# Destination rows gathered beside the first pass of a two-layer graph network, and half of the dense centring on ScalarE

## What is computed

```python
edge_index = jnp.stack([src, dst])
h = jnp.maximum(_layernorm(x), 0.0)
# layer 0: edge features of h[src] times a small net of the edge, summed per dst;
# cos(angle) * (self product of h) + sin(angle) * (sum through lin2)
x = x + _L0_gnn_ref(h, node_vec1, edge_attr_4, edge_attr_8, ..., src, dst, 16)
h = jnp.maximum(_layernorm(x), 0.0)
# layer 1: edge messages of h[src], summed per dst, one more product, relu
x = x + _L1_gnn_ref(h, edge_attr_4, ..., edge_index)
```

## Time and profile before

| | us |
|---|---|
| median of three runs | 2462.75 |
| the profiled execution | 2464.93 |
| its span, first to last instruction | 2463.1 |

### The profile page before, as it was taken

One profiled execution on the slowest core, in us unless ns is written; L12 is line 12 of the kernel. 1 busy time (PEld: TensorE's weight loads), 2 busy tenths in 40 slices (PEclk: granted clock), 3 DMA queues, 4 the chain that ended last, 5 costly groups with the idle time before them and its releaser, 6 DMA issues. The chain is left out here.

```text
span 2463.1 us, 51415 instructions
## 1 busy us (share of the span) xinstructions
PE 1773.9 (72%) x12130; PEld 1620.2 (66%) x12130; DVE 1866.4 (76%) x6716; ACT 1350.1 (55%) x3801; POOL 1483.3 (60%) x1436
## 2 busy tenths in 40 slices
PE   6788888888888888888886544545444777777776
PEld 2777777777777777777775544444444666666665
DVE  1799999999999999999996766666664555656554
ACT  2466666666666666666665645555553444444443
POOL 2345455454555545555454777777776777767775
PEclk9999999999999999999998555555555999999999
DMA  5355555555555555555554333333333333333332
GB/s 184 128 188 206 200 192 193 185 205 200 195 194 184 203 200 198 194 182 202 200 201 165 118 107 113 113 116 121 116 107 93 99 97 105 108 102 109 108 105 72
DMA packets 162656, 376.27 MB, mean 153 GB/s; under 512 B 42142, under 2 KB 72092, under 8 KB 162462
## 3 DMA queue, kind: packets, MB, share of 16 engines
q1 hardware_dynamic: 115582, 301.58, 34.7%
q0 software_dynamic: 47040, 74.31, 11.4%
HBM read 182.72 MB, written 200.80 MB: 156 GB/s over the span
## 5 line engine op out<-in xcount | busy, mean ns | idle before, releaser
L651 POOL TENSOR_TENSOR yo<-x,h 128x640 f32<-128x640 f32 x196 | 303.7, 1550 | 506.0 <-ACT h L774 504.8
L985 PE MATMUL bank<-wp,hT 128*128 128x160 f32 x1568 | 376.3, 322 | 0.0
L774 ACT ACTIVATE h<-x,nmr,inv 128x160 f32<-128x160 f32 x784 | 342.1, 514 | 1.5 <-DVE nmr L1211 1.5
L985 PE MATMUL bank<-wp,eT 128*128 128x160 f32 x784 | 263.6, 429 | 49.9 <-ACT eR L897 43.7
L610 POOL DMA_INDIRECT out<-yo,i_put x196 | 209.1, 1067 | 119.2 <-issue 80.7
L604 POOL DMA_INDIRECT x_e<-in_xa,i_src x196 | 217.3, 1109 | 98.7 <-issue 47.2
L1354 DVE SCALAR_TENSOR_TENSOR x<-bank,scl,x_all 128x160 f32<-128x160 f32 x784 | 256.3, 365 | 5.1 <-PE bank L986 2.6
L610 POOL DMA_INDIRECT h_all<-h,i_put x196 | 223.9, 1142 | 59.8 <-issue 58.6
L986 PE MATMUL bank<-wp,hR 128*128 128x64 f32 x1568 | 259.3, 247 | 0.0
L986 PEld LDWEIGHTS bank<-wp,hR 128*128 128x128 f32 x1568 | 255.5, 190 | 0.0
L980 PE MATMUL bank<-ident,h_e 128*128 128x128 f32 x392 | 83.6, 351 | 223.4 <-DVE hr_e L1526 223.0
(11 more groups left out here) (163 smaller groups left out, 5537.8 us busy)
## 6 DMA issues: line engine op xcount, KB each, us to landing
x_all<-in_xa SPq DMA_DIRECT2D x98, 644.0 KB, 5.0
h_all<-h SPq DMA_DIRECT2D x98, 640.0 KB, 3.0
out<-yo SPq DMA_DIRECT2D x98, 640.0 KB, 3.4
q_row<-row_tab SPq DMA_DIRECT2D x98, 256.0 KB, 3.6
sum_tab<-tot SPq DMA_DIRECT2D x49, 322.0 KB, 4.2
y_tab<-yo SPq DMA_DIRECT2D x49, 320.0 KB
x<-y_tab SPq DMA_DIRECT2D x49, 320.0 KB
cv<-sum_tab SPq DMA_DIRECT2D x25, 322.0 KB, 3.1
```

Source lines behind the costliest of these rows:

```text
L651: nc.gpsimd.tensor_tensor(yo[j][:, a:b], x1[j][:, a:b], h1[j][:, a:b], ALU.add).then_inc(d_y, 1)
L774: ins = nc.scalar.activation(h1[j][:, k * D:(k + 1) * D], x1[j][:, k * D:(k + 1) * D], ACT.Relu, bias=nmr2[j][:, k:k + 1], scale=inv2[j][: ...
L985: nc.tensor.matmul(dst_ps, main[:, t * P:(t + 1) * P], wp[:, w:w + D], start=True, stop=False)
```

## The change

- The destination rows are gathered in the first pass: GpSimd's odd step ends with `own_gather(q-1)`, four indirect DMAs into x_d (two buffers), and SP stores them to a table own_tab in DRAM (`own_store`). In the second stage SP loads a quad from own_tab (`p2_own`), and GpSimd scatters only. The indices are copied by VectorE at the end of its odd steps of the first pass, not in the second stage.
- The sum of a tile goes to bank 5 or 6 in place of bank 1, so `dense_tr`, `p1_tr` and `p1_sum` lose their waits for each other's copies; `p1_source` now waits for the copy of the sum four tiles back, `p1_sum` for the features of the tile before it in the order.
- Of each dense unit, the 128 last columns of row groups 4 to 7 are centred on ScalarE (four activations, mean minus x; the copy of that half into hT turns the sign back), the rest stays on VectorE.
- `dense_y` makes four sums of 320 columns in place of two of 640.

```diff
 # SP
+            def own_store(q):
+                j = q.mod(2)
+                sp.wait_ge(o_g[j], q.over(2, 64, 64))
+                sp.dma_start(own_tab[q.times(1)], x_d[j][:, :]).then_inc(o_st[j], 16)
...
                 if v.mod(2) == 1 and (q - 2).within(Q):
                     p1_store(q - 2)
+                    own_store(q - 2)
...
+            def p2_own(q):
+                k = q.mod(4)
+                wait(sp, r_x1, q.times(2, -6))
+                sp.dma_start(x_q[k], own_tab[q.times(1)]).then_inc(r_g[k], 16)
 # GpSimd
+            def own_gather(q):
+                j = q.mod(2)
+                pool.wait_ge(o_ix, q.times(1, 1))
+                wait(pool, o_st[j], q.over(2, 16))
+                gather(xa, x_d[j], XW, i_dst[j], o_g[j])
...
-                    a, b = h * GQ * D, (h + 1) * GQ * D
-                    nc.gpsimd.tensor_tensor(yo[j][:, a:b], x1[j][:, a:b], h1[j][:, a:b], ALU.add).then_inc(d_y, 1)
+                    for k in (2 * h, 2 * h + 1):
+                        a, b = 2 * k * D, 2 * (k + 1) * D
+                        ins = nc.gpsimd.tensor_tensor(yo[j][:, a:b], x1[j][:, a:b], h1[j][:, a:b], ALU.add)
+                    ins.then_inc(d_y, 1)
...
                 if w.mod(2) == 1 and (q + 1).within(Q):
                     p1_centre(q + 1)
                     p1_scale(q + 1)
+                if w.mod(2) == 1 and (q - 1).within(Q):
+                    own_gather(q - 1)
 # ScalarE
+            def dense_centre(u):
+                act.wait_ge(d_ln1, u.times(1, 1))
+                wait(act, d_tr, u.times(2, -2))
+                x, st = x_in[u.mod(4)], st1[u.mod(4)]
+                for k in range(GQ, GD):
+                    ins = nc.scalar.activation(hb[u.mod(2)][:, k * P:(k + 1) * P], x[:, k * XW + 32:k * XW + D], ACT.Identity,
+                                               bias=st[:, k, 1:2], scale=-1.0)
+                ins.then_inc(d_cna, 1)
...
-                nc.scalar.activation(hT[h][:, :], bank[0][:, :], ACT.Relu)
+                nc.scalar.activation(hT[h][:, :], bank[0][:, :], ACT.Relu, scale=-1.0 if h else 1.0)
...
                     dense_root1(u)
+                    dense_centre(u)
                 slot(u, 0)
 # TensorE
                 pe.wait_ge(d_cen, u.times(1, 1))
+                if h:
+                    pe.wait_ge(d_cna, u.times(1, 1))
                 wait(pe, d_hT, u.times(2, h))
-                wait(pe, e_tot, u.times(2, h - 2))
...
                 wait(pe, e_ft, n.times(1, -1))
+                wait(pe, e_tot, n.times(1, -3))
                 b = bank[5 + n.mod(2)]
...
-                wait(pe, d_hT, dense_copied)
+                pe.wait_ge(e_ft, n.times(1, 3) if (n + 2).within(T) else T)
+                total = bank[5 + n.mod(2)][:, 0:CW]
 # VectorE
-                V.tensor_tensor(x3(hb[j], P, GD), x[:, :, 32:D], bc_last(stat(st1[u.mod(4)], GD, 1), P), ALU.subtract)
+                V.tensor_tensor(x3(hb[j], P, GD)[:, 0:GQ, :], x[:, 0:GQ, 32:D], bc_last(stat(st1[u.mod(4)], GQ, 1), P),
+                                ALU.subtract)
...
+                if u.mod(2) == 1 and (q1 - 1).within(Q):
+                    wait(v, o_g[(q1 - 1).mod(2)], (q1 - 1).over(2, 64))
+                    index_copy(i_dst[(q1 - 1).mod(2)], t_gat, q1 - 1, o_ix)
```

More of the change, by code:

```diff
@@ L90, in gnn_kernel @@
     row_tab = scratch("row_tab", (T, P), i32)
+    own_tab = scratch("own_tab", (Q, P, GQ * XW))
     carry_tab = scratch("carry_tab", (T, P))
@@ L189, in gnn_kernel @@
         i_src = two("i_src", [P, GQ], i32)
-        i_dst = four("i_dst", [P, GQ], i32)
+        i_dst = two("i_dst", [P, GQ], i32)
         i_put = four("i_put", [P, GQ], i32)
@@ L197, in gnn_kernel @@
         x_e = two("x_e", [P, GQ * XW])
+        x_d = two("x_d", [P, GQ * XW])
         h_e = sb("h_e", [P, GQ * P])
@@ L266, in gnn_kernel @@
         d_sq1 = sem("dense_root1_ready")
-        d_cen = sem("dense_centred")
+        d_cen = sem("dense_first_half_centred")
+        d_cna = sem("dense_second_half_centred")
         d_tr = sem("dense_h_transposed")
@@ L305, in gnn_kernel @@
         e_st = sem2("p1_sum_stored")
-        r_ix = sem("p2_index_copied")
+        o_ix = sem("own_index_copied")
+        o_g = sem2("own_rows_gathered")
+        o_st = sem2("own_rows_stored")
         r_px = sem("p2_put_copied")
         r_cv = [sem(f"p2_sums_loaded{i}") for i in range(4)]
-        r_g = [sem(f"p2_node_rows{i}") for i in range(4)]
+        r_g = [sem(f"p2_own_rows_loaded{i}") for i in range(4)]
         r_ln1 = sem("p2_moments1")
@@ L517, in _ @@
                 sp.wait_ge(e_st[j], 16 * ((Q + 1 - j) // 2))
+                sp.wait_ge(o_st[j], 16 * ((Q + 1 - j) // 2))
+            sp.wait_ge(d_x1, 4 * U)
+            def p2_own(q):
+                k = q.mod(4)
+                wait(sp, r_x1, q.times(2, -6))
+                sp.dma_start(x_q[k], own_tab[q.times(1)]).then_inc(r_g[k], 16)
             def p2_sums(q):
@@ L529, in p2_step @@
             def p2_step(v):
+                if v.within(Q):
+                    p2_own(v)
                 if (v - 1).within(Q):
@@ L692, in _ @@
                 step(At(0, w))
[L695 to L699, removed]
             def p2_scatter(q):
@@ L706, in p2_scatter @@
                     scatter_tile(h1_all, h1[j][:, t * D:(t + 1) * D], i_put[q.mod(4)], t, r_put[j])
[L709 to L717, removed]
             for j in range(2):
@@ L720, in _ @@
                 pool.wait_ge(d_sto[j], 16 * (U // 2))
-            with pool.Fori(1, Q // 4) as i:
+            with pool.Fori(0, Q // 4) as i:
                 for c in range(4):
-                    p2_step(At(i, c))
-            for w in range(Q - 1, Q + 4):
-                p2_step(At(0, w))
+                    p2_scatter(At(i, c))
+            p2_scatter(At(0, Q - 1))
             for j in range(2):
@@ L1064, in p1_source, with p1_sum @@
                                  start=True, stop=True).then_inc(e_pw, 1)
-            def p1_sum(n, dense_copied):
+            def p1_sum(n):
                 j, t = n.c // GQ % 2, n.mod(4)
@@ L1072, in p1_sum @@
                 wait(pe, e_tot, n.times(1))
-                wait(pe, d_hT, dense_copied)
+                pe.wait_ge(e_ft, n.times(1, 3) if (n + 2).within(T) else T)
+                total = bank[5 + n.mod(2)][:, 0:CW]
                 before = tot[j][:, (t - 1) * CW:t * CW] if t else tot[1 - j][:, (GQ - 1) * CW:GQ * CW]
-                nc.tensor.matmul(bank[1][:, U_SEG:U_SEG + CW], same[j][:, t * P:(t + 1) * P], v_e[n.mod(2)][:, :],
+                nc.tensor.matmul(total, same[j][:, t * P:(t + 1) * P], v_e[n.mod(2)][:, :],
                                  start=True, stop=False)
-                nc.tensor.matmul(bank[1][:, U_SEG:U_SEG + CW], carry[j][:, t * P:(t + 1) * P], before,
+                nc.tensor.matmul(total, carry[j][:, t * P:(t + 1) * P], before,
                                  start=False, stop=True).then_inc(e_seg, 1)
@@ L1103, in slot @@
                 if (s - 3).within(T):
-                    p1_sum(s - 3, u.times(2, h) if u.within(U) else 2 * U)
+                    p1_sum(s - 3)
             def step(u):
@@ L1514, in p2_stats @@
                 j = q.mod(2)
-                v.wait_ge(r_g[q.mod(4)], q.over(4, 64, 64))
+                v.wait_ge(r_g[q.mod(4)], q.over(4, 16, 16))
                 for pair in range(GQ // 2):
@@ L1663, in p2_step @@
                     p2_angle(q, 7)
-            for q in range(3):
-                index_copy(i_dst[q], t_gat, At(0, q), r_ix)
             v.wait_ge(d_y, 2 * U)
```

6 lines of the change are left out of this document (1 added, 5 removed).

## The result

The changed kernel takes 2445.51 us (median of six runs, 2438.85 to 2457.62) where the kernel before takes 2463.86 on the same chip: a ratio of 0.9935, 95% interval 0.9918 to 0.9952. So it is 18 us faster, and the forecast of 2408 gave 55. The profiled execution has a span of 2443.7 us.

What follows compares the result with a forecast made beforehand. It took a loop per pair through GpSimd, VectorE, TensorE and ScalarE to bound the first pass, and GpSimd the second stage. 2463.1 - 143.8 + 84 + 5.5 = 2408.8, + 1.8 - 2.2 = 2408 us; range 2335 to 2485.

Steps and rivals of the forecast that it cites:

- Second stage: GpSimd's gathers there give way to straight loads on SP's queue, a step takes 7.6 us: -143.8 us.
- rival C: Second stage held at 9 us a step by SP's loads or ScalarE's table loads: +62, 2470 us; chance 0.07.
- GpSimd decides: First pass: own gathers delay `yo`, for which VectorE's x1 waits: +1.8 us a pair, +84 us.
- The leg: GpSimd's stretch per pair, from `yo` before centring to `yo` after the gathers: from 12.45 to 17.45 us.
- The way back: First pass, from x1 over features, TensorE, hT and h to `yo`: from 12.65 to 9.87 us a pair.
- rival B: The way back keeps its length through ScalarE's new activations: +4.55 us a pair, 2538 us; chance 0.12.
- Rival A: First pass: GpSimd gets through its gathers, other engines stay the limit, a unit takes 12.25 us: 2269 us; chance 0.10.
- Centring on ScalarE: First pass: takes 0.53 us a unit off VectorE and gives ScalarE 1.6 us a unit.
- the ring: First pass, closed chain per pair of GpSimd's leg, x1 and the way back: from 25.62 to 27.4 us.
- rival D: First pass: VectorE's subtractions stretch two more gathers a pair, the leg 1.6 us longer: +75, 2483 us; chance 0.05.
- The half-sized `yo`: First pass: each sum split into two of 320 columns pays start-up twice, +0.3 us on the leg.
- The ends: End of the first pass and SP's first load of the second stage: VectorE starts later, +5.5 us.

Runs made afterwards that it cites:

- e7: The kernel before with only the dense part of the change, destination rows still gathered in the second stage: 2326.8 us, 0.9444 of before.
- e3: The changed kernel plus 32 unused transposes on TensorE in even steps, before the product that waits for x1: 2378.5 us, 0.9660 of before.
- e2: The changed kernel with all centring back on VectorE, ScalarE's four activations gone: 2473.7 us, 1.0049 of before.
- e4: The changed kernel with own gathers moved: two behind the even step's sums, two between the odd step's: 2190.2 us, 0.8890 of before.
- e9: The kernel before with sums in bank 5 or 6 and TensorE's three waits for ScalarE's copies removed: 2382.0 us, 0.9665 of before.
- e1: The changed kernel with `yo` again as whole sums of 640 columns: 2442.8 us, 0.9922 of before.
- e11: The kernel before with only `yo` parted, four sums of 320 columns instead of two of 640: 2439.1 us, 0.9918 of before.
- e6: e4 with all centring back on VectorE, ScalarE's activations gone: 2280.3 us, 0.9254 of before.
- e8: e4 with the source gathers parted too, two before the even step's first half of `yo`, two between its halves: 2194.2 us, 0.8910 of before.
- e12: e4 with `yo` again as two whole sums of 640 columns: 2180.1 us, 0.8852 of before.
- e5: The changed kernel with two of the four own gathers moved, one to each of e4's two places: 2253.5 us, 0.9148 of before.

## Why the prediction was right and where it failed

- *Second stage*, -143.8: measured -141.7, a quad every 7.6 us. Right, and so rival C didn't come. e7 shows that the gathers alone make it.
- *GpSimd decides*: right. x1 waits for `yo` once a pair, the selector is 0.68 us long. The leg of 17.45, 17.52 up to x1, measured 17.67. (The source gathers of the second pair shown are 0.61 us longer than those of the first, not 0.8; the rest is the pause before them.)
- *The way back*, 9.87: the term that failed. It was made of durations of the kernel before, in which TensorE works at a granted clock of 1.00. The forecast itself made TensorE wait for x1 once a pair, and priced its work behind that wait as if it had not. It also goes from the end of the features (1020.28) straight to hT's 3.44 us, which begin with the transposes at 1021.62, and leaves out the 1.34 us between without a word. At full clock both are about right: in e3 the gap is 0.15 us in the mean and the path to hT 3.26. At the lower clock behind the idle time the dense products are still running when the features are ready: the gap is 1.07 us in the mean, and the path to hT 3.89. The part from x1 to the features was 0.4 shorter than forecast (3.45). Per pair the way back is 1.0 over the forecast, and 1.5 over e3; of the 123.8 us that the pass lost, e3 has 58.5 (its x1 run from 81.2 to 1382.9).
- *Its rival B* named a longer way back, but for ScalarE's activations, and put the sign's turn at 28.7 us a pair. Measured were 28.56, and 18 us were left: near its turn, as it said, but ScalarE was not the cause. The way back of e2, without ScalarE's activations, is the same (10.91).
- *Rival A*, 2269: its premise, a ring that doesn't hold, is what e4 builds, and that takes 2190. The price of 12.25 us a unit was wrong. x1 in e4 run from 81.6 to 1197.1, 11.5 a unit. I had let the removed waits for ScalarE's copies count 0.1 a unit; e9 shows 0.8. The 2269 was 79 us too high.
- *Centring on ScalarE*: the 0.53 us of VectorE were counted as a gain only without the ring. By e2 it is worth 28 us with it. What I put as rival D, gathers stretched by VectorE's subtractions, is real: own gathers take 1.11 us in the mean against 0.95 for the source gathers, 0.65 us a pair, of which the 5.3 us of the forecast held about 0.3. It was not the 1.6 of the rival.
- *The half-sized `yo`*, +0.3 on the leg: +0.27 in the sums, mostly given back by shorter gathers, so 0.1 (e1).
- *The ends*: +5.5 forecast, +3.8 measured. Right.
- *The range*, 2335 to 2485: its low end follows from the ring's bound of +10, but the bound of +210 would have put the high end at 2534.

Two misses of about 65 us and 25 us have opposite signs: the clock cost more than nothing, and the ring at full clock was shorter than forecast (58.5 instead of 84 us over the pass). That the second hid over a third of the first was luck. What stays open: the last 4 us at the end of the kernel, which of the moved sums and waits shorten the subtraction in e9 and e11, how the costs of e6 add up, and in e8 why the subtraction, whose record begins 0.4 us before the sum's, comes second.

The best version, e12, is the change with the own gathers in GpSimd's idle stretches and the sum whole: 2180.1 us, 0.8852 of before.

## What to carry to other kernels

An engine that is half idle isn't free at every place of its program: ask which wait follows the inserted work, and put it where the engine was waiting anyway; here that decided between 0.7% and 11%. When a forecast opens an idle stretch on TensorE, work out the sum with the work behind it at half the clock too, since durations read from a kernel without such a stretch may not hold: 4.2 us idle in each pair did it here, and e5, in which TensorE has no such stretch, kept its clock. A short wait that recurs four times in a ring and stands on an engine with little slack is a large term, so count it per turn.

## What the runs showed of the hardware

- In the turn shown TensorE is idle for 3.76 us, and its granted clock is 0.60 in the next 3 us, in which it falls, and 0.50 in the 3 after that: the two 160-column products above take 0.90 instead of 0.44 us. With the idle time filled (e3) the clock is 1.00.
- A 512-column VectorE instruction with both inputs in SBUF that meets a sum of GpSimd ends 0.55 us after it, and two sums in a row count as one: 2.02 and 2.65 us in the meetings shown instead of 0.68. The Trainium skill (SBUF — State Buffer, "SBUF: two separate sides") calls this an exclusive lock of a shared port pair, held for a whole instruction. The trace agrees on the length of the wait.
- Gathers don't hold the selector up: in the changed kernel it overlaps one each time and takes 0.67 to 0.69 us, 38 times. Gathers are held up by VectorE's instructions with two inputs in SBUF: 0.95 us where they meet none, 1.43 in the mean for the own gathers of the changed kernel that meet both subtractions, 1.82 in e2, where the first of these is 1.21 us long (200 to 1100 us).
